# Additive attention: five relus on VectorE, four on ScalarE, and other places in a tile for roots, exponential, scores and sums

## The reference

```python
e = relu(sqrt(relu(q_i + k_j) + eps) - sqrt(relu(-(q_i + k_j)) + eps))   # for all i, j: 1024 x 1024 x 64
scores = einsum('bija,a->bij', e, Wphi)
ex = exp(scores - max_j scores);  denom = sum_j ex
part1 = einsum('bij,bjc->bic', ex, Vy)
Ew = einsum('bij,bija->bia', ex, e);  part2 = Ew @ We.T + We_b * denom
out = (part1 + part2) / (denom + 1e-9)
```

## Time and profile before

| | us |
|---|---|
| Median of 3 runs | 6201.85 (6200.22 to 6207.91) |
| Profiled execution, own time | 6189.22 |
| Its span, first to last instruction | 6187.5 |
| PE, DVE, ACT, POOL busy over the span | 5159.3, 4349.8, 3649.9, 2995.0 |

### The profile page before, as it was taken

One profiled execution on the slowest core, in us unless ns is written; L12 is line 12 of the kernel. 1 busy time (PEld: TensorE's weight loads), 2 busy tenths in 40 slices (PEclk: granted clock), 3 DMA queues, 4 the chain that ended last, 5 costly groups with the idle time before them and its releaser, 6 DMA issues. The chain is left out here.

```text
span 6187.5 us, 90222 instructions
## 1 busy us (share of the span) xinstructions
PE 5159.3 (83%) x30328; PEld 2655.2 (43%) x30328; DVE 4349.8 (70%) x6797; ACT 3649.9 (59%) x2416; POOL 2995.0 (48%) x2483
## 2 busy tenths in 40 slices
PE   5866868579975888888989888988988888769999
PEld 2323323247752334333434333333333343347777
DVE  2848567443332899999999999999998999832221
ACT  1010110220014899998999898989898989534443
POOL 1514325001102666666666666667666766323333
PEclk9989889779987999999999999999999999779999
DMA  1000000000011000000000000000000000110000
GB/s 76 0 0 0 0 0 0 32 0 10 10 48 64 3 2 3 2 3 14 2 3 2 3 2 15 2 3 2 3 9 4 2 3 2 48 37 14 14 14 7
DMA packets 37278, 70.89 MB, mean 11 GB/s; under 512 B 4592, under 2 KB 22224, under 8 KB 34384
## 3 DMA queue, kind: packets, MB, share of 16 engines
q1 hardware_dynamic: 35024, 62.60, 2.9%
q0 software_dynamic: 2176, 7.34, 0.3%
HBM read 50.00 MB, written 19.92 MB: 11 GB/s over the span
## 5 line engine op out<-in xcount | busy, mean ns | idle before, releaser
L808 DVE CUSTOM_DVE_ANT_0 e_slots<-e_slots,banks 128x1024 f32<-128x1024 f32 x2048 | 2461.6, 1217 | 272.6 <-PE banks L524 260.9
L595 ACT ACTIVATE e_slots<-e_slots 128x4096 f32<-128x4096 f32 x512 | 1842.6, 3617 | 168.8 <-DVE e_slots L755 83.5
L524 PE MATMUL banks<-ex_parts,sel 128*128 128x512 f32 x4096 | 1568.4, 466 | 224.6 <-DVE ew L808 135.5
L488 PE MATMUL banks<-e_slots,w_score 128*32 128x256 f32 x16384 | 1387.3, 413 | 158.2 <-ACT e_slots L595 151.2
L657 POOL TENSOR_SCALAR e_slots<-k,qt 128x1024 f32<-128x1024 f32 x896 | 1020.6, 1141 | 868.6 <-DVE ew L808 799.6
L663 POOL TENSOR_SCALAR e_slots<-e_slots,qt 128x1024 f32<-128x1024 f32 x896 | 1014.9, 1141 | 64.4 <-POOL e_slots L657 25.7
L524 PEld LDWEIGHTS banks<-ex_parts,sel 128*128 128x128 f32 x4096 | 650.4, 200 | 840.4 <-DVE ew L808 592.1
L586 ACT ACTIVATE e_slots<-k,qt 128x1024 f32<-128x1024 f32 x768 | 856.2, 1141 | 130.5 <-DVE ew L808 120.8
L488 PEld LDWEIGHTS banks<-e_slots,w_score 128*32 128x32 f32 x16384 | 333.6, 111 | 918.9 <-issue 700.7
L1746 POOL TENSOR_TENSOR g_l<-tmp,g_h 128x512 fp32r<-128x512 f32 x192 | 248.7, 1295 | 436.1 <-ACT g_h L1713 307.1
L755 DVE TENSOR_SCALAR e_slots<-k,qt 128x1024 f32<-128x1024 f32 x384 | 422.3, 1153 | 0.0
(11 more groups left out here) (270 smaller groups left out, 6583.7 us busy)
## 6 DMA issues: line engine op xcount, KB each, us to landing
stage<-in_h SPq DMA_DIRECT2D x8, 1024.0 KB, 4.8
x_tokens<-in_x SPq DMA_DIRECT2D x1, 4096.0 KB, 18.3
w_down<-in_w_down SPq DMA_DIRECT2D x1, 4096.0 KB, 13.2
x_between<-x_tokens SPq DMA_DIRECT2D x8, 512.0 KB, 3.1
kx<-x_between SPq DMA_DIRECT2D x8, 512.0 KB, 4.6
v_all<-v_out POOLq DMA_DIRECT2D x8, 512.0 KB, 3.2
vy<-v_all SPq DMA_DIRECT2D x4, 1024.0 KB, 6.2
xg<-x_between SPq DMA_DIRECT2D x32, 128.0 KB, 2.5
```

What stands on the lines that cost most here:

```text
L488: ins = nc.tensor.matmul(banks[TI * g:TI * (g + 1), par, side * QW:(side + 1) * QW], c_["w_score"][:, s, half, :], e_slots[:, par, COLG * ...
L524: ins = nc.tensor.matmul(spread[n % 2][:, half * W:(half + 1) * W], c_["sel"][:, half, n, :], ex_parts[:, par, :], start=True, stop=True)
L595: nc.scalar.activation(e_slots[:, par, four, :], e_slots[:, par, four, :], ACT.Sqrt, bias=EPS_RHO).then_inc(sqrt_done, 1)
L808: nc.vector.tensor_tensor_reduce(out=e, in0=e, in1=spread[n % 2], scale=1.0, scalar=0.0, op0=ALU.mult, op1=ALU.add, accum_out=ew[:, q, pla ...
```

## The change

- `Z_BY`: GpSimd keeps seven relus (0, 1, 4, 5, 7, 8, 9), ScalarE has four (2, 3, 6, 10) in place of six, VectorE five (11 to 15) in place of three, all five behind reduction 15.
- ScalarE's `step` becomes: root 3 of tile t + 1; relus 2, 3, root 0 and relu 6 of tile t + 2; the exponential of tile t + 1; relu 10, table load, roots 1 and 2 of tile t + 2. The start makes tile 0's roots and root 0 of tile 1, then the first exponential.
- GpSimd's `step`: relus 0, 1, then 4, 5, then 7, 8 of tile t + 2, parts of tile t + 1, then relu 9.
- Scores: no piece in places 0, 8, 9, 14, 15; four pieces (4 to 7, tile t + 1) in place 1, then 1, 2, 1, 2, 1, 1 in places 2 to 7; pieces 0 to 3 of tile t + 2 in places 10 to 13.
- The turn of the exponentials moves from place 1 to 0. The 24 sums take other places: twelve in places 8 to 15 of the last tile, twelve in 0, 2 and 8 to 12 of the next.

```diff
-    Z_BY = "PPAAAPPAPPAAPVVV"
-    Z_AFTER = {15: [13, 14, 15]}
-    EXT_AT, EXT_AT_FIRST, MAX_AT, END_AT = 1, 13, 8, {14: (1,), 15: (2, 3)}
-    SUMS_AT = 4
-    SCORES_AT = {0: (1, 7), 1: (1, 8), 2: (1, 9), 3: (1, 10), 4: (1, 11), 5: (1, 12), 6: (1, 13), 7: (1, 14), 8: (1, 15),
-                 9: (2, 0), 10: (2, 1), 11: (2, 2), 12: (2, 3), 13: (2, 4), 14: (2, 5), 15: (2, 6)}
+    Z_BY = "PPAAPPAPPPAVVVVV"
+    Z_AFTER = {15: [11, 12, 13, 14, 15]}
+    EXT_AT, EXT_AT_FIRST, MAX_AT, END_AT = 0, 13, 8, {14: (1,), 15: (2, 3)}
+    SUMS_LAST, SUMS_NEXT = {8: 2, 9: 2, 10: 1, 11: 1, 12: 1, 13: 1, 14: 2, 15: 2}, {0: 2, 2: 1, 8: 3, 9: 3, 10: 1, 11: 1, 12: 1}
+    SCORES_AT = {1: (1, (4, 5, 6, 7)), 2: (1, (8,)), 3: (1, (9, 10)), 4: (1, (11,)), 5: (1, (12, 13)), 6: (1, (14,)), 7: (1, (15,)),
+                 10: (2, (0,)), 11: (2, (1,)), 12: (2, (2,)), 13: (2, (3,))}
...
+            def first_root(t, par, freed):
+                for n in (2, 3):
                     relu(t, par, n, freed)
                 sqrt(t, par, 0)
-                relu(t, par, 7, freed)
+                relu(t, par, 6, freed)
+
+            def next_roots(t, par, freed):
+                relu(t, par, 10, freed)
+                nc.scalar.preload_act_table(ACT.Sqrt)
                 sqrt(t, par, 1)
+                sqrt(t, par, 2)
+
+            def last_root(t, par):
+                sqrt(t, par, 3)
             def step(t, par):
+                last_root(t + 1, 1 - par)
+                first_root(t + 2, par, t * NP)
                 ex_of(t + 1, 1 - par)
-                later_roots(t + 2, par, t * NP)
-                first_roots(t + 3, 1 - par, (t + 1) * NP)
...
-                for some in ((0, 1), (5, 6), (8, 9), (12,)):
+                for some in ((0, 1), (4, 5), (7, 8), (9,)):
                     some_z(par, par, some, None)
...
                     some_z(t + 2, par, (0, 1), t * NP)
-                    some_z(t + 2, par, (5, 6), t * NP)
-                    some_z(t + 2, par, (8, 9), t * NP)
+                    some_z(t + 2, par, (4, 5), t * NP)
+                    some_z(t + 2, par, (7, 8), t * NP)
                 pool.wait_ge(bc_done, t * NP)
                 parts(t + 1, 1 - par)
                 if not last:
-                    some_z(t + 2, par, (12,), t * NP)
+                    some_z(t + 2, par, (9,), t * NP)
```

More of the change, by code:

```diff
@@ L421, in adaln_kernel @@
         TILES, GROUPS, N_SUMS = B * NTI, B * NG, (1 + CC) * JT
+        N_LAST = sum(SUMS_LAST.values())
+        assert N_LAST + sum(SUMS_NEXT.values()) == N_SUMS
         def sp_c(sp):
@@ L519, in tile @@
                 par = q % 2
+                i_sum = 0
                 pe.wait_ge(parts_done, t + 1 + 1)
@@ L534, in tile @@
                     ins.then_inc(bc_done, 1)
-                    ahead, m = SCORES_AT[n]
+                    ahead, ms = SCORES_AT.get(n, (0, ()))
                     if not (last and q >= GT - ahead):
-                        scores(t + ahead, m, (q + ahead) % 2)
-                    if sums_of is not None and n >= SUMS_AT:
-                        if n == SUMS_AT:
-                            pe.wait_ge(vy_loaded, values)
-                        sums(sums_of, n - SUMS_AT)
-                    if more_sums_of is not None and NP - SUMS_AT + n < N_SUMS:
-                        sums(more_sums_of, NP - SUMS_AT + n)
+                        for m in ms:
+                            scores(t + ahead, m, (q + ahead) % 2)
+                    if sums_of is not None:
+                        for _ in range(SUMS_LAST.get(n, 0)):
+                            if i_sum == 0:
+                                pe.wait_ge(vy_loaded, values)
+                            sums(sums_of, i_sum)
+                            i_sum += 1
+                    if more_sums_of is not None:
+                        for _ in range(SUMS_NEXT.get(n, 0)):
+                            sums(more_sums_of, N_LAST + i_sum)
+                            i_sum += 1
             def group_on(tg, values, last=False):
@@ L552, in group_on @@
                 else:
-                    for i in range(NP - SUMS_AT, N_SUMS):
+                    for i in range(N_LAST, N_SUMS):
                         sums(tg, i)
@@ L557, in pe_c @@
                 scores(0, m, 0)
-            for m in range(SCORES_AT[0][1]):
-                scores(1, m, 1)
+            for n in range(NP):
+                if n in SCORES_AT and SCORES_AT[n][0] == 2:
+                    for m in SCORES_AT[n][1]:
+                        scores(1, m, 1)
             tile(0, 0)
@@ L602, in ex_of @@
                 nc.scalar.activation(ex[:, :], bank(par), ACT.Exp, bias=negmax[:, 0:1]).then_inc(exp_done, 1)
[L604 to L612 removed]
+            def first_root(t, par, freed):
+                for n in (2, 3):
                     relu(t, par, n, freed)
                 sqrt(t, par, 0)
[L615 removed]
+                relu(t, par, 6, freed)
+            def next_roots(t, par, freed):
+                relu(t, par, 10, freed)
+                nc.scalar.preload_act_table(ACT.Sqrt)
                 sqrt(t, par, 1)
+                sqrt(t, par, 2)
+            def last_root(t, par):
+                sqrt(t, par, 3)
             def step(t, par):
+                last_root(t + 1, 1 - par)
+                first_root(t + 2, par, t * NP)
                 ex_of(t + 1, 1 - par)
[L621 to L626 removed]
+                next_roots(t + 2, par, t * NP)
+            first_root(0, 0, None)
+            next_roots(0, 0, None)
+            last_root(0, 0)
+            first_root(1, 1, None)
             ex_of(0, 0)
[L628 to L629 removed]
+            next_roots(1, 1, None)
+            with act.Fori(0, TILES // 2 - 1) as u:
                 step(u * 2, 0)
                 step(u * 2 + 1, 1)
[L632 to L634 removed]
+            last_root(TILES - 1, 1)
             ex_of(TILES - 1, 1)
```

16 lines of the change are left out of this document (removed).

## The result

| | before | after |
|---|---|---|
| Median | 6201.03 us (4 runs, 6194.17 to 6207.91) | 6086.49 us (4 runs, 6086.15 to 6094.78) |
| Profiled execution, own time | 6189.22 | 6094.78 |
| Its span | 6187.5 | 6093.1 |
| The phase (rows 1, and below) | 3359.8 | 3274.2 |
| One group of four tiles | 105.0 | 102.3 |

The ratio is 0.9818, with a 95% interval of 0.9801 to 0.9835: the change saves 114.5 us; 60 were forecast. On the profiled executions the span fell by 94.4: 85.6 inside the phase, the rest mostly from its start, which comes 10 us earlier.

A forecast was written before the change was run, and what follows sets the result against it. No engine is full; hand-overs bound the loop. A group of 101.3 + 1.9 + 0.3 = 103.5 us against 105.0 saves 48 us, the start 12: 60 in all, median 6142 us, range 6055 to 6260.

The forecast's parts named there:

- rival (c): Whole group: no low clock left and the tile-by-tile estimate holds, 130 us saved, 6072 us; chance 0.18.
- Relus of VectorE: Block behind a tile's last reduction: five relus cost 3.3 us alone, 6.7 beside GpSimd, which should be done by then.
- contention: GpSimd still running beside VectorE's relus: some 0.3 us of delay, priced at 0.2 us in each of three tiles.
- ScalarE: ready: ScalarE has 21.8 us of work a tile and waits 1.8 us or more ahead of the exponential.
- rival (e): ScalarE sets the pace with 24.5 us of work a tile in place of 21.8: 6180 us; chance 0.02.
- The walk of an ordinary tile: Step-by-step timing of VectorE and TensorE through one tile's reductions: a period of 23.62 us, tile 3 24.23.
- Tile 0: First tile of a group, with `sums_of_e`, extra sums and the turn at place 13: 27.03 us.
- The clock behind a group's end: TensorE idles 3.8 us there and falls to 1.2 GHz in every group: 1.9 us a group, bounds 0 and 3.3.
- The clock at the other seams: Between the other tiles four pieces fill TensorE's waiting time, so low clock costs only 0.3 us a group.
- Rival (a): TensorE's low clock stays as frequent at the other seams or comes more often: +120 us, 6262; chance 0.17.
- quick groups: Groups of four tiles in the old kernel taking 102.0 us at granted clock 0.97; slow ones 107.5 at 0.90.
- The start: Start of the phase: the first exponential no longer waits for eight roots, 12 us net saved, bounds 8 and 15.

The follow-up runs named there:

- e4: Changed kernel with three more GpSimd operations on a dead buffer behind its last relu of each tile: 6221.11 us, ratio 1.0036.
- e8: Changed kernel with the row maximum one reduction later and one score piece in each of places 4 to 8: 6104.75 us, ratio 0.9841.
- e1: Changed kernel with six thrown-away score pieces behind the four of place 1 in tile 1 of each group: 6044.30 us, ratio 0.9753.
- e10: Changed kernel with the group's end earlier, plus score pieces 0 to 3 moved to places 12 to 15 and tile 3's sums shifted: 6149.16 us, ratio 0.9916.
- e6: Changed kernel with the old split: relus 11 and 12 back on ScalarE, three on VectorE: 6195.31 us, ratio 0.9990.
- e2: Kernel before with three thrown-away score pieces ahead of the one in place 1 in tiles 1 to 3: 6102.01 us, ratio 0.9845.
- e7: Changed kernel with the 24 sums back one each in places 4 to 15 and 0 to 11: 6153.98 us, ratio 0.9926.

## Why the prediction was right, and where it was mis-sized

The sign and the mechanism held: five relus in 3.4 us because GpSimd is done. The size didn't: 114.5 us saved where 60 were forecast. The time lies nearer to rival (c), 6072, than to the forecast, but (c)'s mechanism, no low clock left, did not come: 2.7 us a group are left in tile 1. Step by step:

- **Relus of VectorE: right, and without the contention that I added.** The block is 3.4 us in 125 of the 126 tiles that have one. The 0.2 us in each of three tiles for a late GpSimd did not appear: 0.6 a group too much, 19 us. The margin is as thin as the prediction said, since e4's and e8's blocks, with GpSimd longer or later by a little, take 4.0 to 4.5. The "6.7 us" for five relus beside GpSimd was an end that nothing reached; with its whole relu beside them they took 5.36, because GpSimd's relu ends before they do. The prediction also took the old price, 4.08 us for three, for three tiles of four; behind tile 3 it was 2.93.
- **ScalarE: ready.** It waited 2.2 us per exponential, 1.8 or more was forecast. By the Trainium skill, ScalarE: Activation LUTs, section What ACT_TABLE_LOAD costs, a switch is 2.66 us; two switches a tile would have left nothing of that wait. The trace doesn't agree here: the load starts at 2176.93 and the root at 2178.22, 1.29 us for the switch, as the rows below show, and rival (e) falls.

```profile
2175.18 0.69 ACT L613 ACTIVATE ex<-banks,negmax 128x512 f32<-128x512 f32 x1 [1.74 <-DVE negmax L783]
...
2176.93 1.28 ACT L623 ACT_TABLE_LOAD   x1
2178.22 3.63 ACT L606 ACTIVATE e_slots<-e_slots 128x4096 f32<-128x4096 f32 x1
```

- **The walk of an ordinary tile: right to 0.04 us.** 23.62 forecast, 23.58 measured; tile 3 24.23 forecast, 24.16 measured. Reductions 4 to 8 start 1.19, 1.23, 1.66, 1.23, 1.24 behind the one before them; the walk has 1.22, 1.23, 1.71, 1.23, 1.23.
- **Tile 0: mis-sized by 1.0 us a group, 32 us.** 29.3 by the walk (27.0 and the 2.27 of the group's end, counted from first reduction to first reduction), 28.3 measured. Two terms were too high. Three sums in a row cost 0.59 us from their start to the next spread (2218.61 to 2219.20), not 3 x 0.25. And one small step of the group's end takes 0.22 us now; it took 0.65 to 0.77 before in 31 of 32 groups, beside a relu of GpSimd's that now ends ahead of it. Before, then after (timelines of DVE and POOL, after with TensorE's sums):

```profile
2142.45 1.12 POOL L657 TENSOR_SCALAR e_slots<-k,qt 128x1024 f32<-128x1024 f32 x1
...
2142.88 0.77 DVE L781 TENSOR_SCALAR rden<-den 128x128 f32<-128x128 f32 x1
```

```profile
2125.90 1.12 POOL L675 TENSOR_SCALAR e_slots<-e_slots,qt 128x1024 f32<-128x1024 f32 x1 [0.20 <-POOL e_slots L669]
...
2127.15 0.22 DVE L793 TENSOR_SCALAR rden<-den 128x128 f32<-128x128 f32 x1
...
2218.61 0.83 PE L505 MATMUL banks<-ex_t,vy 128*128 128x128 f32 x6
...
2219.20 0.70 PE L528 MATMUL banks<-ex_parts,sel 128*128 128x512 f32 x2
```

- **The clock behind a group's end: right in its place, too small.** 1.9 us forecast (bounds 0 to 3.3), 26.3 - 23.6 = 2.7 measured, 26 us in all. It does not always start in the idle time, as the prediction had it: in 12 groups it starts in the tail of tile 0, at the same cost. I had counted half of the low time as cost, less slack; but the low stretch covers places 1 to 3, where the spread that the reductions wait for comes directly behind idle time, so that hardly any slack is left. e1 shows the price: where its filler held the clock, tile 1 is 23.6.
- **The clock at the other seams: nearly gone, as forecast,** 0.3 us a group forecast, 0 measured in tiles 2 and 3. Rival (a) didn't come with this order. Low stretches ahead of full places did come in e10, and at other seams in e6, with other orders of the same work.
- **Where the gain is: the low clock for the most part, as forecast, but the order gains too.** The shortest tiles of the old kernel, with 23.6 for tile 1 where e2's filler holds the clock, make 28.0 + 23.6 + 23.9 + 25.0 = 100.5 us a group without low clock; the new one's make 28.3 + 23.6 + 23.6 + 24.2 = 99.7. So low clock cost 105.0 - 100.5 = 4.5 a group and costs 102.3 - 99.7 = 2.6 now: 1.9 of the 2.7 saved. The forecast had 101.3 for a group at full clock, slower than the old one's by this measure, since it compared with quick groups of 102.0, in which the low clock of the group's end is still contained; the order in truth gains 0.8, nearly all in tile 3, where the sums left places 4 to 7 (e7).
- **The start: 8.5 us in place of 12.** The first reduction comes at 2005.85, 10.0 us earlier (near 2002 was forecast), and tile 1's first reduction 8.5 earlier. Two roots of tile 0 wait for GpSimd at the start, 4.23 and 3.38 us, where the old kernel's first two waited 3.19 and 0.70. After, then before (ScalarE's timelines):

```profile
1972.12 3.62 ACT L606 ACTIVATE e_slots<-e_slots 128x4096 f32<-128x4096 f32 x1 [4.23 <-POOL e_slots L675]
...
1982.50 3.62 ACT L606 ACTIVATE e_slots<-e_slots 128x4096 f32<-128x4096 f32 x1 [3.38 <-POOL e_slots L675]
```

```profile
1968.98 3.62 ACT L595 ACTIVATE e_slots<-e_slots 128x4096 f32<-128x4096 f32 x1 [3.19 <-POOL e_slots L663]
...
1974.34 3.62 ACT L595 ACTIVATE e_slots<-e_slots 128x4096 f32<-128x4096 f32 x1 [0.70 <-POOL e_slots L663]
```

  The second root needs slot 7, which ScalarE made itself before and GpSimd makes now: a hand-over that the walk did not ask about. These 3.7 us are the miss. Of the 2 us that I took off for the root of tile 1, 1.5 came.

Summed: contention 19, tile 0 32, clock -26, other seams 10, start -4: 31 of the 34 us by which the profiled execution was under its forecast (6094.8 for 6129.2). The other 20 us to the median are the profiled execution's own place among the runs: of before it lay 12.6 under the median, of after 8.3 above it.

## What to carry to other kernels

A split of work among engines and the order in each engine's list are one edit: here each half alone gave nothing or cost 5%, since the one decides which root waits for which relu and the other decides who runs beside whom. Ask of each long block on VectorE what GpSimd does in that time, and of each idle time of TensorE what work comes directly behind it, because that work can run at 1.2 GHz: behind the 4.20 us of a group's end it did, behind the 1.56 us of the ordinary seams it didn't. Thrown-away work in such a gap is a probe before it is a cure: look at what else it moves. Put the low stretch where it is hidden (beside the relus, in the tail of tile 0) before you try to remove it: moving the group's end ahead of the last reduction gave 50 us more than the change, with not one instruction less.
